# Two graph layers on one core: the check of group sizes moves to GpSimd between the passes, row numbers move to the drain, first-pass gathers wait only for their buffer

## The chip, the cores and the metric

One core of a Trainium2 chip runs the program. Its engines are TensorE (PE, with weight loads shown apart as PEld), VectorE (DVE), ScalarE (ACT), GpSimd (POOL) and SyncE (SP); each runs its own list of instructions and waits for the others on semaphores. ACT and SP also issue DMAs (ACTq, SPq), and GpSimd issues the gathers, which are DMAs that take their row numbers from a tile. The metric is the device time of one execution in microseconds, as the median of several.

## What is computed

100,000 nodes with 64 features, 50,000 edges with 32 attributes, edges given as `src` and `dst`, `dst` ascending.

```python
h = relu(layernorm(x))                                   # only x's shape matters to layer 0 here
# layer 0: over the edges of each src node
seg_sum, seg_max = segment_sum(edge_attr, src), segment_max(edge_attr, src)
seg_mean = seg_sum / max(cnt, 1);  seg_max = where(cnt > 0, seg_max, 0)
x = x + relu(concat[seg_sum, seg_max, seg_mean, u[0]] @ W1 + b1) @ W2 + b2
# layer 1
h = relu(layernorm(x))
x = x + relu(segment_sum(h[src], dst) @ W.T + b)
```

## The kernel before

**Before the passes** (0 to 186 us of the trace) the edges' `src` numbers are sorted on VectorE, the sorted positions are turned into row numbers for the gathers (`gi[0]`), and rows of flags for the scans are stored.

**The first pass** (layer 0) goes over 98 blocks (`BLOCKS`) of 512 sorted edges. For block n: GpSimd gathers the edges' attributes into a ring of eight buffers `xa` (`gather_attr`, four gathers of 128 rows, L540). VectorE multiplies them by a share (`scale_attr`, L1060), TensorE turns them (`turn_attr`, L1355), VectorE runs two scans over them (`scans`, L1072 and L1074), TensorE multiplies by W1 (L1360), ScalarE applies relu (`hidden`, L677), TensorE multiplies by W2 (L1367), VectorE writes the record (`less_constant`, L1122), ScalarE stores it in DRAM. Two blocks later SP and ACT load windows of 112 records for groups of 128 nodes (`windows` on SP, `upper_windows` on ACT, L667); VectorE copies their keys into PSUM (`keys_to_psum`, L1085) and makes 0/1 matrices (`onehots`, L1095), TensorE adds records up by node with them (`expand`, L1379, after one or two matmuls of ones that only fill time, L1384), and VectorE adds the node's own row (`add_dense`, L1114). SP stores the result as the table T.

These steps are software-pipelined by hand. VectorE's loop runs n from 0 to 104; its body at n is: scans(n), add_dense(n-7), keys_to_psum(n-5), scale_attr(n+2), onehots(n-5), less_constant(n-1). So from n = 98 on there is nothing left to scan, and the last seven bodies are the **drain**. When every row of T is stored, SP raises `table_ok`.

**The second pass** (layer 1) gathers rows of T by `gi[1]` (`gather_x`, L559), in the same manner, and ends the program. It is one arm of a choice: `fast` is 1 where no group has more than 112 edges and the row bounds hold; the other arm is a slow way for other inputs, not taken here. All five engines read `fast` before the second pass.

**What the choice needs.** `start_f` and `near_f` are rows of 800 group starts on one partition, for `src` and `dst`. From them `group_starts` (L839) makes the first pass's window addresses, `dst_group_starts` (L829 to L834) the second pass's, `start_row[1]`, and its share of the checks; `group_checks` (L844 to L848) is the rest of the checks. They stand in VectorE's loop at n = 3, 10 and 13. `permute(gi[1], 3, 7)` at n = 9 (L877 to L880) turns `src` numbers into T's row numbers. At n = 15 VectorE sums the counts of wrong items, TensorE adds them over the partitions (L1398), and VectorE writes `fast` (L1157).

**What paces the gathers.** `gather_attr(n)` waits at its first gather until buffer n-8 has been turned. Its second gather also waits for the scans of block n-4 (`feats_ok`), its third and fourth for `added` and `hot_ok` of earlier blocks.

## Time and profile before

| what | us |
|---|---|
| median of 3 runs (lowest, highest) | 1256.63 (1252.74, 1262.65) |
| the profiled execution | 1261.67 |
| its span in the trace | 1259.8 |
| VectorE busy in the span | 1030.1 (82%) |
| TensorE busy | 960.6 (76%) |
| GpSimd busy | 758.0 (60%) |
| ScalarE busy | 280.1 (22%) |
| TensorE's granted clock, mean (share of full) | 0.888 |

The span is the time from the first to the last event that the trace shows; the execution's own time is 1.9 us longer. A share over the whole span mixes four stages: sorting (0 to 186 us), the first pass (186 to 699), its drain (699 to 731) and the second pass (731 to 1260). Each must be read by itself. In rows of the timeline, a bracket gives the idle time of the engine ahead of the instruction and what ended it; "issue" means that nothing the profile shows was waited for.

### The profile page before, as it was taken

How to read it: one execution, taken by the hardware profiler on the slowest of the kernel's cores; microseconds unless marked ns; L12 is line 12 of the kernel's file. 1: busy time of each engine (PE TensorE's matmuls, PEld its weight loads, DVE VectorE, ACT ScalarE, POOL GpSimd, SP SyncE). 2: the span in 40 equal slices, each digit the busy share in tenths (PEclk: the TensorE clock that was granted, in tenths of full speed). 3: DMA queues.
4: the chain of work that ended last, by engine and by line, in shares of the span. 5: the costliest groups of instructions: out<-in, count | busy, mean ns of one | idle time of the engine just before them, and what ended most of it. 6: DMA issues, size and time to landing. Idle time of an engine off the chain costs nothing.

```text
span 1259.8 us, 20767 instructions
## 1 busy us (share of the span) xinstructions
PE 960.6 (76%) x5818; PEld 758.0 (60%) x5818; DVE 1030.1 (82%) x2727; ACT 280.1 (22%) x681; POOL 758.0 (60%) x821
## 2 busy tenths in 40 slices
PE   0131027979999999999999823879889788888888
PEld 0010014757777777777777613767767677677777
DVE  8888887899999999999999624777777777777774
ACT  1441042212222222222222101112112112111110
POOL 3000046667777777777776067777777777777750
PEclk9995556889999999999999955898999989988899
DMA  2000012767899888888888654777788778777775
GB/s 65 0 0 0 0 53 68 175 161 206 236 232 240 234 226 219 241 220 236 230 222 240 164 173 98 180 201 203 210 222 207 202 198 210 210 208 201 203 186 156
DMA packets 317563, 218.51 MB, mean 173 GB/s; under 512 B 223428, under 2 KB 255140, under 8 KB 317444
## 3 DMA queue, kind: packets, MB, share of 16 engines
q1 hardware_dynamic: 182100, 135.41, 38.7%
q10 hardware_dynamic: 110256, 62.42, 18.8%
q0 software_dynamic: 25088, 19.32, 8.6%
q8 instruction: 47, 0.77, 0.3%
q14 instruction: 72, 0.59, 0.1%
HBM read 137.51 MB, written 79.45 MB: 172 GB/s over the span
## 4 chain that ended last, share of the span: by engine, by line
DVE 36%; POOL 20%; DMA 13%; PE 11%; issue 10%; ACTq 5%; ACT 2%; SPq 0%; POOLq 0%; DVEq 0%
POOL xa L559 11%; POOL xa L540 9%; DMA xa<-node_table,gi 8%; DMA win<-records 5%; DVE feats L1074 4%; DVE feats L1072 4%; ACTq L667 3%; DVE oneh L1095 3%; DVE dout L1114 2%; PE p_m L1367 2%; DVE kb L920 2%; DVE ka L920 2%; DVE shared L1095 2%; DVE ka L921 2%; DVE kb L921 2%
## 5 line engine op out<-in xcount | busy, mean ns | idle before, releaser
L540 POOL DMA_INDIRECT xa<-in_edge_attr_dram,gi x392 | 375.2, 957 | 252.3 <-issue 115.4
L559 POOL DMA_INDIRECT xa<-node_table,gi x392 | 369.9, 944 | 158.7 <-issue 105.8
L677 ACT ACTIVATE hid<-p_z,bias_z 128x512 f32<-128x512 f32 x98 | 113.4, 1157 | 249.2 <-issue 230.0
L1408 PE MATMUL p_g<-ident,hn 128*128 128x128 f32 x196 | 46.6, 325 | 106.9 <-DVE hn L1182 106.5
L1074 DVE TENSOR_TENSOR_SCAN feats<-c_rows,feats,p_g 32x512 f32<-32x512 f32 x97 | 123.3, 1271 | 1.4
L1095 DVE SCALAR_TENSOR_TENSOR shared<-p_m,node_of 112x1024 f32<-112x1024 f32 x98 | 117.1, 1195 | 6.8 <-PE p_z L1379 3.4
L1072 DVE TENSOR_TENSOR_SCAN feats<-c_rows,feats,p_g 64x512 f32<-64x512 f32 x97 | 122.5, 1263 | 0.1
L1367 PE MATMUL p_m<-w_s,hid 128*128 128x64 f32 x784 | 109.3, 284 | 15.8 <-ACT hid L677 15.4
L730 ACT ACTIVATE sd<-mv,eps_t 128x4 f32<-128x4 f32 x98 | 29.1, 297 | 413.2 <-DVE mv L1173 350.4
L1095 DVE SCALAR_TENSOR_TENSOR oneh<-p_m,node_of 112x1024 f32<-112x1024 f32 x98 | 119.3, 1217 | 0.2
L1360 PE MATMUL p_z<-feats,w_s 96*128 96x512 f32 x196 | 112.4, 657 | 6.2 <-DVE feats L1074 6.2
L1168 DVE BATCH_NORM_STATS2 stat<-xa 128x6 f32<-128x64 f32 x392 | 58.7, 212 | 67.6 <-DMA xa<-node_table,gi 63.9
L1379 PEld LDWEIGHTS p_u<-win,oneh 128*128 128x128 f32 x784 | 97.1, 195 | 26.9 <-issue 22.5
L1384 PE MATMUL p_t<-one 128*128 128x256 f32 (+1 forms) x228 | 112.5, 578 | 0.0
L1379 PEld LDWEIGHTS p_t<-win,oneh 128*128 128x128 f32 x784 | 96.4, 194 | 25.5 <-issue 24.1
L1384 PE MATMUL p_u<-one 128*128 128x512 f32 x230 | 110.7, 566 | 0.0
L1367 PEld LDWEIGHTS p_m<-w_s,hid 128*128 128x128 f32 x784 | 97.6, 196 | 21.5 <-ACT hid L677 19.9
L1379 PE MATMUL p_u<-win,oneh 128*128 128x64 f32 x784 | 94.9, 275 | 2.2 <-DVE oneh L1095 2.2
L1408 PEld LDWEIGHTS p_g<-ident,hn 128*128 128x128 f32 x196 | 25.0, 159 | 117.8 <-DVE hn L1182 116.9
L1085 DVE COPY p_m<-win 112x8 f32<-112x8 f32 x196 | 32.8, 167 | 75.9 <-DMA win<-records 75.7
L1379 PE MATMUL p_t<-win,oneh 128*128 128x64 f32 x784 | 93.9, 273 | 0.5 <-DVE oneh L1095 0.5
L1182 DVE SCALAR_TENSOR_TENSOR hn<-xa,mv,p_m 128x64 f32<-128x64 f32 x392 | 83.9, 276 | 3.5
(253 smaller groups left out, 1539.3 us busy)
## 6 DMA issues: line engine op xcount, KB each, us to landing
win<-records SPq DMA_DIRECT2D x980, 28.9 KB
records<-rec ACTq DMA_DIRECT2D x196, 132.0 KB
din<-in_x_dram SPq DMA_DIRECT2D x49, 512.0 KB
node_table<-dout SPq DMA_DIRECT2D x49, 512.0 KB, 3.6
din<-node_table SPq DMA_DIRECT2D x43, 512.0 KB
out_dram<-dout SPq DMA_DIRECT2D x43, 512.0 KB
c_rows<-rows_src ACTq DMA_DIRECT2D x141, 128.0 KB
win<-records ACTq DMA_DIRECT2D x588, 28.9 KB
```

The source lines that it names most:

```text
L540: g.indirect_dma_start(out=xa[n % XRING][:, t, 0:FE], out_offset=None, in_=edge_attr, in_offset=bass.IndirectOffsetOnAxis(ap=gi[0][:, BT * ...
L559: g.indirect_dma_start(out=xa[k % XRING][:, t, :], out_offset=None, in_=T, in_offset=bass.IndirectOffsetOnAxis(ap=gi[1][:, BT * n + t:BT * ...
L677: s.activation(hid[n % 2][:, :].rearrange("p (t n) -> p n t", n=P), p_z[n % 2][:, :].rearrange("p (n t) -> p n t", t=BT), ACT.Relu, bias=b ...
L1072: v.tensor_tensor_scan(f[0:64, :], c[0:64, at:at + BLK], p_g[n % 2][0:64, :], first[0:64], ALU.mult, ALU.add)
L1074: v.tensor_tensor_scan(f[64:96, :], c[64:96, at:at + BLK], p_g[n % 2][0:32, :], first[64:96], ALU.min, ALU.max).then_inc(feats_ok, 1)
L1095: v.scalar_tensor_tensor(hots[side][m % HRING][0:WP, :, :], key_at(k).unsqueeze(2).to_broadcast([WP, PER, UNIT]), -float(STEP * m), node_o ...
L1182: last = v.scalar_tensor_tensor(hn[n % 2][:, t, :], xa[(BLOCKS + n) % XRING][:, t, :], mv[n % 2][:, t, 0:1], up[:, t:t + 1].to_broadcast([ ...
L1360: mm(p_z[n % 2][:, :], w1_s[:, :], feats[n % 2][:, :], start=True, stop=True).then_inc(z_ok, 1)
L1367: last = mm(p_m[0][:, D * t:D * (t + 1)], hid[n % 2][:, P * t:P * (t + 1)], w2_s[:, :], start=True, stop=True)
L1379: last = mm(to[:, D * s:D * (s + 1)], hots[side][m % HRING][:, s, :], win[k % WRING][:, s, 0:D], start=True, stop=True)
L1384: mm(bank[:, 0:width], one[:, :], one[:, :].unsqueeze(1).to_broadcast([P, width // P, P]), start=True, stop=True)
L1408: last = tr(p_g[n % 2][:, P * h:P * (h + 1)], hn[n % 2][:, 2 * h:2 * h + 2, :].rearrange("p t d -> p (t d)"), ident[:, :])
```

## The change

- The waits of `gather_attr` for `feats_ok`, `added` and `hot_ok` go. The wait for the buffer stays.
- `dst_group_starts` and `group_checks` go from VectorE. After its last first-pass gather has landed and after the preset of `hot1`, GpSimd now makes `over`, `over2` and `start_row[1]` from `start_f`, `near_f` and `limit` in 15 instructions of one partition by 800 or 784, each waiting for the one before, and raises `s_over`.
- `permute(gi[1], 3, 7)` moves on VectorE from n = 9 to n = 99.
- The choice moves from n = 15 to n = 101 (`CHOICE`), on VectorE and on TensorE. On VectorE it now begins with a wait for `s_over` and two sums over 784 numbers.

```diff
+CHOICE = BLOCKS + 3
             def gather_attr(n):
-                behind = n - LEAD
                 for t in range(BT):
                     if t == 0 and n >= XRING:
                         pool.wait_ge(turned, n - XRING + 1)
-                    if t == 1 and valid(behind):
-                        pool.wait_ge(feats_ok, behind + 1)
-                    elif t == 2 and valid(behind - SRC_ADD):
-                        pool.wait_ge(added, behind - SRC_ADD + 1)
-                    elif t == 3 and valid(behind - SRC_HOT):
-                        pool.wait_ge(hot_ok, behind - SRC_HOT + 1)
...
+            pool.wait_ge(s_near, 2)
+            pool.wait_ge(s_cast, 2)
+            for side, (row, more) in enumerate(((start_f, over), (near_f, over2))):
+                link(g.tensor_scalar(room[:, :], row[:, :], float(-ROW), None, ALU.mult))
+                link(g.tensor_tensor(room[:, :], room[:, :], limit[:, :], ALU.add))
+                link(g.tensor_scalar(more[:, :], room[:, :], 0.0, None, ALU.is_lt))
+                if side == 1:
+                    link(g.tensor_scalar(room[:, :], room[:, :], 0.0, None, ALU.max))
+                    link(g.tensor_tensor(room[:, :], limit[:, :], room[:, :], ALU.subtract))
+                    link(g.tensor_copy(start_row[1][:, :], room[:, :]))
+                link(g.tensor_tensor(room[:, 0:LAST], row[:, 1:LAST + 1], row[:, 0:LAST], ALU.subtract))
+                link(g.tensor_scalar(room[:, 0:LAST], room[:, 0:LAST], float(WP), None, ALU.is_gt))
+                last = g.tensor_tensor(more[:, 0:LAST], more[:, 0:LAST], room[:, 0:LAST], ALU.add)
+                if side == 0:
+                    link(last)
+            last.then_inc(s_over, 1)
             pool.wait_ge(s_fast, 1)
...
+            def choice():
+                dve.wait_ge(s_over, 1)
+                v.reduce_sum(wrong[0:1, 0:1], over[:, 0:LAST], AX.X)
+                v.reduce_sum(wrong[0:1, 1:2], over2[:, 0:LAST], AX.X)
+                v.tensor_scalar(wrong[0:1, 4:5], start_f[:, LAST:LAST + 1], float(E), None, ALU.not_equal)
+                link(v.tensor_scalar(wrong[0:1, 5:6], near_f[:, LAST:LAST + 1], float(E), None, ALU.not_equal))
+                v.reduce_sum(wrong1[:, :], wrong[:, :], AX.X).then_inc(s_wrong, 1)
+                dve.wait_ge(s_wsum, 1)
+                v.tensor_scalar(fast[:, :], p_m[1][0:1, 0:1], 0.0, None, ALU.is_equal).then_inc(s_fast, 1)
...
-                if n == 9:
+                if n == 3:
+                    group_starts()
+                if n == BLOCKS + 1:
                     dve.wait_ge(s_dcols, 16)
                     permute(gi[1], 3, 7)
                     v.tensor_copy(rowmax[:, :], eps_t[:, :]).then_inc(s_drows, 1)
-                if n == 3:
-                    group_starts()
-                if n == 10:
-                    dst_group_starts()
-                if n == 13:
-                    group_checks()
-                if n == 15:
-                    v.reduce_sum(wrong1[:, :], wrong[:, :], AX.X).then_inc(s_wrong, 1)
-                    dve.wait_ge(s_wsum, 1)
-                    v.tensor_scalar(fast[:, :], p_m[1][0:1, 0:1], 0.0, None, ALU.is_equal).then_inc(s_fast, 1)
+                if n == CHOICE:
+                    choice()
...
-                if n == 15:
+                if n == CHOICE:
                     pe.wait_ge(s_wrong, 1)
```

The order of GpSimd's instructions in the middle of the first pass, before the change; `xa3` to `xa4` are buffers of the ring, and the bracket names the semaphore waited for:

```order
L540 DMA xa3<-in_edge_attr_32_dram,gi0 128x32 [waits turned]
L540 DMA xa3<-in_edge_attr_32_dram,gi0 128x32 [waits feats_ok]
L540 DMA xa3<-in_edge_attr_32_dram,gi0 128x32 [waits added]
L540 DMA xa3<-in_edge_attr_32_dram,gi0 128x32 [waits hot_ok]
L540 DMA xa4<-in_edge_attr_32_dram,gi0 128x32 [waits turned]
L540 DMA xa4<-in_edge_attr_32_dram,gi0 128x32 [waits feats_ok]
L540 DMA xa4<-in_edge_attr_32_dram,gi0 128x32 [waits added]
L540 DMA xa4<-in_edge_attr_32_dram,gi0 128x32 [waits hot_ok]
```

The same place with the change:

```order
L536 DMA xa3<-in_edge_attr_32_dram,gi0 128x32 [waits turned]
L536 DMA xa3<-in_edge_attr_32_dram,gi0 128x32 x3
L536 DMA xa4<-in_edge_attr_32_dram,gi0 128x32 [waits turned]
L536 DMA xa4<-in_edge_attr_32_dram,gi0 128x32 x3
L536 DMA xa5<-in_edge_attr_32_dram,gi0 128x32 [waits turned]
L536 DMA xa5<-in_edge_attr_32_dram,gi0 128x32 x3
```

Three of four waits are gone; the one for the buffer stands.

VectorE's instructions from body 99 to body 102 of its loop, with the change (L1117 is the adding of the node's row, L1088 the copy of keys, L1098 the 0/1 matrix, L1125 the record):

```order
L1117 TENSOR_TENSOR dout<-p_t,din 128x512 [waits dense_out0_1,dense_in0_0,expanded]
L1088 COPY p_m<-win 112x8 [waits win_in_2]
L1098 SCALAR_TENSOR_TENSOR oneh<-p_m,node_of 112x1024 [waits window_keys_in_psum]
L880 TENSOR_SCALAR tm<-gi 128x512 [waits dst_columns]
L881 TENSOR_SCALAR td<-gi 128x512
L882 SCALAR_TENSOR_TENSOR gi<-gi,tm 128x512 [waits vector_step]
L883 TENSOR_TENSOR gi<-gi,td 128x512 [waits vector_step]
L1152 COPY rowmax<-eps_t 128x1 [waits vector_step]
L1117 TENSOR_TENSOR dout<-p_u,din 128x512 [waits expanded]
```

```order
L1098 SCALAR_TENSOR_TENSOR oneh<-p_m,node_of 112x1024 [waits window_keys_in_psum]
L845 TENSOR_REDUCE wrong<-over 1x1 [waits groups_checked]
L846 TENSOR_REDUCE wrong<-over 1x1
L847 TENSOR_SCALAR wrong<-start_f 1x1
L848 TENSOR_SCALAR wrong<-near_f 1x1
L849 TENSOR_REDUCE wrong<-wrong 128x1 [waits vector_step]
L851 TENSOR_SCALAR fast<-p_m 1x1 [waits wrong_summed]
L1117 TENSOR_TENSOR dout<-p_u,din 128x512 [waits expanded]
L1088 COPY p_m<-win 112x8 [waits win_in_1]
```

The first piece is the permutation behind the 0/1 matrix of block 94, the second the choice behind that of block 96. Before the change these places held only L1114, L1085 and L1095.

TensorE's last instructions of the first pass with the change (L1381 fills time, L1376 is the adding up by node, of blocks 95, 96 and 97):

```order
L1381 MATMUL p_u<-one 128x512
L1376 MATMUL p_u<-win,oneh 128x64 x8
L1395 MATMUL p_m<-one,wrong 1x1
L1381 MATMUL p_t<-one 128x512
L1376 MATMUL p_t<-win,oneh 128x64 x8
L1381 MATMUL p_u<-one 128x512
L1376 MATMUL p_u<-win,oneh 128x64 x8
```

The sum over the partitions (L1395) now stands between the adding up of blocks 95 and 96, and nothing behind it on TensorE can begin until VectorE has counted.

## Rows read from the trace of the kernel before

**Rows 1.** Stages: busy us (instructions) of PE, PEld, DVE, ACT, POOL, PEclk, DMA share, GB/s

```profile
295.00:456.00 161.00, 160.54 (x1045) 125.55 (x1043) 159.42 (x228) 44.33 (x65) 121.08 (x128) 1.00 0.90 233
699.00:731.00 32.00, 24.01 (x146) 18.41 (x144) 16.71 (x25) 3.97 (x5) 0.21 (x1) 0.89 0.66 181
```

**Rows 2.** Timeline of VectorE, first scan of blocks 8, 9, 17, 97: start us, us

```profile
236.62 1.26 DVE L1072 TENSOR_TENSOR_SCAN feats<-c_rows,feats,p_g 64x512 f32<-64x512 f32 x1
241.55 1.26 DVE L1072 TENSOR_TENSOR_SCAN feats<-c_rows,feats,p_g 64x512 f32<-64x512 f32 x1
...
295.14 1.26 DVE L1072 TENSOR_TENSOR_SCAN feats<-c_rows,feats,p_g 64x512 f32<-64x512 f32 x1
...
699.07 1.26 DVE L1072 TENSOR_TENSOR_SCAN feats<-c_rows,feats,p_g 64x512 f32<-64x512 f32 x1
```

**Rows 3.** Timeline of VectorE, what stands in bodies 9 to 15 besides the loop

```profile
246.47 0.47 DVE L877 TENSOR_SCALAR tm<-gi 128x512 int32<-128x512 int32 x1
...
248.75 0.15 DVE L1147 COPY rowmax<-eps_t 128x1 f32<-128x1 f32 x1
...
253.80 0.97 DVE L829 SCALAR_TENSOR_TENSOR start_row<-near_f,limit 1x800 int32<-1x800 f32 x1
...
257.59 0.96 DVE L833 TENSOR_REDUCE wrong<-over 1x1 f32<-1x784 f32 x1
...
289.82 0.15 DVE L1157 TENSOR_SCALAR fast<-p_m 1x1 int32<-1x1 f32 x1 [0.28 <-PE p_m L1398]
```

**Rows 4.** A stage of 4 us, columns as in rows 1

```profile
280.00:284.00 4.00, 3.04 (x7) 1.74 (x8) 3.97 (x7) 0.00 (x0) 2.22 (x3) 0.54 0.66 164
```

**Rows 5.** Timeline of TensorE and of VectorE, after the checks

```profile
280.96 2.07 PE L1360 MATMUL p_z<-feats,w_s 96*128 96x512 f32 x2 [2.29 <-DVE feats L1074]
```

```profile
269.03 0.42 DVE L1122 TENSOR_TENSOR rec<-p_m,c_neg 128x256 f32<-128x256 f32 x1 [0.67 <-PE p_m L1367]
...
289.05 0.42 DVE L1122 TENSOR_TENSOR rec<-p_m,c_neg 128x256 f32<-128x256 f32 x1 [1.09 <-PE p_m L1367]
```

**Rows 6.** Waits of GpSimd, 165 to 700 us: total, times, longest

```profile
POOL xa L540 <- DVE feats L1074: 24.0, 21, 4.2
```

**Rows 7.** Timeline of GpSimd: first and last first-pass gather, preset, first second-pass gathers

```profile
170.87 1.16 POOL L540 DMA_INDIRECT xa<-in_edge_attr_dram,gi  x1 [112.92 <-ACT gi L697]
...
684.47 0.95 POOL L540 DMA_INDIRECT xa<-in_edge_attr_dram,gi  x1 [0.30 <-issue]
689.21 2.13 POOL L570 COPY shared<-ident 32x1024 f32<-32x1024 f32 x2 [3.79 <-issue]
730.79 0.97 POOL L559 DMA_INDIRECT xa<-node_table,gi  x1 [39.46 <-SPq L416]
```

**Rows 8.** Timeline of VectorE: the multiplication by the share

```profile
477.12 0.29 DVE L1060 TENSOR_TENSOR xa<-xa,share 128x128 f32<-128x128 f32 x1 [0.47 <-DMA xa<-in_edge_attr_dram,gi]
...
690.88 0.60 DVE L1060 TENSOR_TENSOR xa<-xa,share 128x128 f32<-128x128 f32 x1
```

**Rows 9.** Timeline of GpSimd at the start

```profile
4.38 1.41 POOL L496 IOTA limit_i<- 1x800 int32 x1
...
15.90 0.35 POOL L517 TENSOR_SCALAR_AFFINE_SELECT shifted<-shifted 128x130 f32<-128x130 f32 x1
```

**Rows 10.** Timeline of the drain, VectorE and then TensorE

```profile
717.09 1.22 DVE L1095 SCALAR_TENSOR_TENSOR oneh<-p_m,node_of 112x1024 f32<-112x1024 f32 x1
...
721.86 0.17 DVE L1085 COPY p_m<-win 112x8 f32<-112x8 f32 x1 [2.95 <-DMA win<-records]
```

```profile
718.37 2.00 PE L1379 MATMUL p_t<-win,oneh 128*128 128x64 f32 x16 [0.51 <-DVE oneh L1095]
720.20 1.08 PE L1384 MATMUL p_u<-one 128*128 128x512 f32 x2
723.35 3.08 PE L1379 MATMUL p_u<-win,oneh 128*128 128x64 f32 x16 [2.07 <-DVE oneh L1095]
```

**Rows 11.** The page's costliest groups: second-pass gathers

```profile
L559 POOL DMA_INDIRECT xa<-node_table,gi x392 | 369.9, 944 | 158.7 <-issue 105.8
```

More of the change, by code:

```diff
@@ L178, in build @@
         near_f = sb("near_f", [1, GROUPS])
+        room = sb("room", [1, GROUPS])
         wrong = sb("wrong", [P, 6])
@@ L238, in build @@
         s_wrong = sem("wrong_counted")
+        s_over = sem("groups_checked")
         s_wsum = sem("wrong_summed")
@@ L823, in rows_above @@
                 v.tensor_tensor(in_group[:, :], less[:, 1:SPAN + 1], less[:, 0:SPAN], ALU.subtract).then_inc(s_above, 1)
-            def dst_group_starts():
-                dve.wait_ge(s_near, 1)
-                dve.wait_ge(s_cast, 2)
-                v.scalar_tensor_tensor(start_row[1][:, :], near_f[:, :], float(ROW), limit[:, :], ALU.mult, ALU.min)
-                v.scalar_tensor_tensor(over2[:, :], near_f[:, :], float(ROW), limit[:, :], ALU.mult, ALU.is_gt)
-                link(v.tensor_tensor(over[:, 0:LAST], near_f[:, 1:LAST + 1], near_f[:, 0:LAST], ALU.subtract))
-                link(v.scalar_tensor_tensor(over[:, 0:LAST], over[:, 0:LAST], float(WP), over2[:, 0:LAST], ALU.is_gt, ALU.add))
-                link(v.reduce_sum(wrong[0:1, 1:2], over[:, 0:LAST], AX.X))
-                link(v.tensor_scalar(wrong[0:1, 5:6], near_f[:, LAST:LAST + 1], float(E), None, ALU.not_equal))
             def group_starts():
@@ L839, in group_starts @@
                 v.scalar_tensor_tensor(start_row[0][:, :], start_f[:, :], float(ROW), limit[:, :], ALU.mult, ALU.min).then_inc(s_start, 1)
-            def group_checks():
-                last = LAST
-                link(v.scalar_tensor_tensor(over2[:, :], start_f[:, :], float(ROW), limit[:, :], ALU.mult, ALU.is_gt))
-                link(v.tensor_tensor(over[:, 0:last], start_f[:, 1:last + 1], start_f[:, 0:last], ALU.subtract))
-                link(v.scalar_tensor_tensor(over[:, 0:last], over[:, 0:last], float(WP), over2[:, 0:last], ALU.is_gt, ALU.add))
-                v.reduce_sum(wrong[0:1, 0:1], over[:, 0:last], AX.X)
-                link(v.tensor_scalar(wrong[0:1, 4:5], start_f[:, last:last + 1], float(E), None, ALU.not_equal))
+            def choice():
[7 more added lines that the diff above has]
+                v.tensor_scalar(fast[:, :], p_m[1][0:1, 0:1], 0.0, None, ALU.is_equal).then_inc(s_fast, 1)
             def beside_turn(t):
```

## The prediction

> **What bounds the kernel now.** I read the busy time by stages first. In the clean part of the first pass (295 to 456 us) VectorE is busy 159.4 of 161 us, at full TensorE clock, while TensorE shows 160.5 and GpSimd 121.1 [rows 1]. TensorE's figure counts overlapping ends and matmuls that only fill time, so it does not decide; the timeline does: VectorE begins block 9's scan 4.93 us after block 8's [rows 2], back to back, and that is the loop's period. From block 17 to block 97 it takes 403.9 us, 5.05 us a block [rows 2]: 80 x 4.93 = 394.4, so 9.5 us are stalls spread over that stretch. From block 9 to block 17, eight blocks, it takes 53.6 us where 39.4 would do [rows 2]: 14.2 us too much. The code that the change moves stands in this stretch. Of GpSimd, 392 gathers at 0.94 us and a gap of 0.30 (the bracket of its rows) are about 1.25 us each, 5.0 us a block, a little slower than VectorE's 4.93. It took from 170.87 to 685.4 [rows 7], 514.5 us, of which 24.0 in 21 waits for VectorE's scans [rows 6]; each of those would have had the ordinary gap of 0.3 anyway, so 17.7 us are real waiting.
>
> The second pass begins at `table_ok`: the first gather stands at 730.79 [rows 7]. There GpSimd is idle 158.7 us in all for 392 gathers, 39.5 of it ahead of the first [rows 7, 11]; the other 119.2 us are 0.30 us a gather, the plain gap. So it issues without ever truly waiting, and the second pass starts and ends later or earlier as a whole with `table_ok`.
>
> **The work that leaves the loop.** The permutation runs from 246.47 to the end of its small copy at 248.9: 2.4 us. The six instructions for `near_f` run from 253.80 to 258.55 and one small one of 0.15: 4.9 us. The five for `start_f` are four of 0.96 us and a small one: 4.0 us. The choice is two of 0.15 and a wait of 0.28, 0.6 us [rows 3]. Together 11.9 us. VectorE also lost 0.67 us at 269.03 and 1.09 us at 289.05 waiting for TensorE [rows 5]. These I count as consequences: while VectorE checks, TensorE has no scan to multiply, stands idle 2.29 us, and then runs at a mean granted clock of 0.54 (nearly all at the 1.2 GHz level), the pair of L1360 taking 2.07 us [rows 4, 5]. Without the checks it has no such gap. 11.9 + 1.8 is 13.7 of the 14.2; the remaining 0.5 has the same neighbourhood. I take **-14.2 us**; if the slow-clock waits stayed, -11.9.
>
> **The gathers.** They now wait for nothing but a buffer turned eight blocks ago. At 5.0 us a block from 170.87 GpSimd would be done at 661 to 668, instead of 685.4, and its rows landed some 3.8 us later (685.4 to the preset at 689.2, which waits for them) [rows 7]: by 672 at the latest. VectorE needs block 97's rows at 690.88 [rows 8], 15 us sooner with the savings, at about 676. So GpSimd stays ahead to the end, by 4 us or more, and no buffer wait arises, since it is never eight blocks ahead. What this removes on VectorE's side is waits like the 0.47 us at 477.12 [rows 8] and what follows from them; I count **-1.0**, between 0 and -1.5. Most of the 9.5 us of stalls are not waits for gathers and I leave them where they are. The loop's saving would be lost in part without this edit: gathers at 5.0 us a block that also wait for scans have only the slack of rows 8.
>
> **The check on GpSimd.** 15 instructions on one partition, none of which the trace shows. Bounds for one: the preset's copy, 1,024 elements in half of 2.13 us [rows 7], is 0.83 us for 800; the slowest per element is L517, 130 elements in 0.35 us, which is 2.15 us for 800 [rows 9]. The one row of this very shape, one partition by 800, is L496's 1.41 us [rows 9]; I take it, 15 x 1.41 = 21 us (12 to 32). They start when the last gather has landed (667 to 672) and the preset's 2.1 us are over, so `s_over` comes at about 690 to 695. VectorE asks for it after block 96's 0/1 matrix, which ended at 718.3 [rows 10] and now ends at 703. It is hidden, by 8 us or more; it begins to cost where one instruction takes over about 2.2 us, so the cover holds on the whole range but barely at its end.
>
> While these run, VectorE still multiplies by the share for the last two blocks. In rows 8 this instruction took 0.60 us instead of 0.29, at 690.88, beside the second of the two copies of rows 7, and ended about when the copy did; the scans beside them kept their 1.26 to 1.27. Two such instructions, each held for about half of a 1.0 to 1.4 us instruction, less the 0.31 paid now: **+0.7** (0 to +2). The Trainium skill states this, in "SBUF — State Buffer", section "Who interferes with whom": a VectorE instruction with both inputs in SBUF contends with a GpSimd instruction that reads SBUF, and one with at most one input there does not. By that rule, the trace agrees: 0.60 against 0.29 for the one, no change for the scans, which read PSUM.
>
> **The drain.** The permutation comes in after block 94's matrix, in a place where VectorE waits for windows anyway: at most 0.6 us late for the next, made good by the wait for the window of block 96; **+0.1**. The choice comes at 718.3 (old clock): two sums of 0.96, three small ones, a matmul and its wait: about 3.0 us until `fast`. On VectorE that fills the 2.95 us of waiting for block 97's window [rows 10] and costs 0.1. TensorE pays more. It ran block 96's adding up at 718.37, in 2.00 us, and filled time at 720.20, so that block 97's could begin at 723.35 [rows 10]. Now block 96 must wait for the count, until about 720.9, with an idle gap of 3.4 us ahead. Then come fill (0.9), 16 matmuls (1.8), fill (0.9), 16 matmuls (1.9), ending at 726.4: at full clock nothing is lost against 723.35 + 3.08 = 726.43. If TensorE is at half clock throughout, it is 1.7 + 3.1 + 1.7 + 3.1 = 9.6 us, ending at 730.5, +4.1. A shorter gap, 2.29 us, was followed by the low clock [rows 4, 5], so I put it nearer that end: **+2.7** (0.1 to 4.1). Reading `fast` is late too, but `table_ok` is another 7 us behind.
>
> **Sum.** -14.2 - 1.0 + 0.7 + 0.1 + 2.7 = **-11.7 us**. The profiled execution had 1261.67 us, so 1250.0 for it; it stood 5.0 us above the median of the runs, 1256.63, and against that the time is **1245 us**, 0.9% faster. The ends of the terms (-11.9 or -14.2; 0 or -1.5; 0 or 2; 0.2 or 4.2) make -15.5 to -5.7, that is 1241 to 1251.
>
> **Rivals.**
> (a) *The spread stalls go too.* The 9.5 us of stalls after block 17 may come from gathers that arrive just in time: in rows 8 a wait for a gather stands among them, and the stretch 295 to 456, with the gathers ahead, has almost none (159.4 of 161 us busy). With GpSimd ahead throughout, 8 us more would go: 1237. Against it: I see most of them as late records, behind ScalarE's issue of window loads.
> (b) *The earlier gathers bring stalls to where there were none.* They come at other moments, and the DMA share is already 0.90 [rows 1]. Stalls at the rate of the second half (some 7 us in 43 blocks) over the 32 clean ones would cost 5 us: 1250.
> (c) *Slower.* The count comes late and holds the drain. The time is lost one for one from 2.2 us an instruction on; the gain is used up at 2.2 + 11.7/15 = 3.0 us, and at 3.85 us, 58 us for the 15, the time is over 1% longer, 1269. For it: nothing like these instructions is in the trace. Against it: it would have to be nearly twice the dearest row.
> The Trainium skill, "GPSIMD Engine Reference", section "Performance versus the Vector engine", speaks against putting elementwise work there, about twice VectorE's time; its 4497 ns for 2,048 elements of two inputs would be 1.76 us for 800, an estimate of 26 us if all 15 cost that. By it the count is ready at about 700, still ahead of 703, and the sum stays; that rule makes (c) thin cover but no loss. No run here shows it yet.
> (d) *Nothing comes of it*: the stretch from block 9 to 17 is held by something else once the checks are gone, GpSimd or ScalarE's issue. Then some 3 us remain: 1253. Rows 2's 4.93 us a block right before it speak against.
>
> **How the numbers follow.** Forecast 0.52, (a) 0.17, (b) 0.18, (c) 0.04, (d) 0.09. About 1% (12.6 us, below 1244.1) is what a measurement can tell from no change. The forecast's 1241 to 1251 lies a third below it; (a) wholly: faster 0.4. Slower than 1269 only in (c)'s far end: 0.03. Same: 0.57. The range reaches from (a) to beyond (b): **1237 to 1254**.
>
> **What would show it.** Right: first scans of blocks 9 to 17 take about 39.5 us; no TensorE clock below 1.0 there; GpSimd's last first-pass gather ends by 668; its checks are over before VectorE's 0/1 matrix of block 96; no wait of L845 for them; a gap of about 3.4 us and slow matmuls on TensorE in the drain; `table_ok` about 12 us sooner, the second pass as long as before (529 us). Wrong: VectorE waiting at L845; L1060's successor waiting for gathers; stalls before block 60.

## The result and the profile after

The changed kernel takes 1248.95 us (median of 15 runs, 1243.64 to 1255.75) against 1257.42 for the kernel before (15 runs, 1252.74 to 1262.89): a ratio of 0.9924, with a 95% interval of 0.9907 to 0.9942. It is 0.8% faster, 9.6 us by the ratio (7.3 to 11.7 by the interval) and 8.5 between the medians. That is less than the 1% which the prediction had taken as its bound, but the interval does not reach 1. Two further timings of the changed kernel, below, gave 0.9931 and 0.9918. Differences in us between timed kernels are worked out from the ratios here.

The profiled execution took 1251.71 us with a span of 1249.8; of before it was 1261.67 and 1259.8. Stages are cut at first scans and at the first second-pass gather. The third column of the table is another execution of the changed kernel, profiled later; its span is nearer to the usual one.

| us | before | changed | changed, third timing |
|---|---|---|---|
| start to block 9's scan | 241.6 | 241.4 | 240.4 |
| block 9 to 17 | 53.6 | 42.3 | 40.2 |
| block 17 to 97 | 403.9 | 401.7 | 401.0 |
| block 97 to the first second-pass gather (drain) | 31.7 | 36.2 | 35.7 |
| from there to the end | 529.0 | 528.2 | 528.2 |
| span | 1259.8 | 1249.8 | 1245.5 |

The timeline of VectorE of the changed kernel (start us, us), first scans of blocks 9, 17 and 97, answers [rows 2]:

```profile
241.39 1.26 DVE L1075 TENSOR_TENSOR_SCAN feats<-c_rows,feats,p_g 64x512 f32<-64x512 f32 x1
...
283.68 1.26 DVE L1075 TENSOR_TENSOR_SCAN feats<-c_rows,feats,p_g 64x512 f32<-64x512 f32 x1
...
685.43 1.26 DVE L1075 TENSOR_TENSOR_SCAN feats<-c_rows,feats,p_g 64x512 f32<-64x512 f32 x1
```

GpSimd's timeline of the same execution, last first-pass gather to first second-pass gather, answers [rows 7] and shows some of the new instructions:

```profile
662.16 1.09 POOL L536 DMA_INDIRECT xa<-in_edge_attr_dram,gi  x1 [0.30 <-issue]
666.75 2.13 POOL L566 COPY shared<-ident 32x1024 f32<-32x1024 f32 x2 [3.50 <-issue]
668.97 2.23 POOL L571 TENSOR_SCALAR room<-start_f 1x800 f32<-1x800 f32 x1
671.28 1.87 POOL L572 TENSOR_TENSOR room<-room,limit 1x800 f32<-1x800 f32 x1
...
675.53 1.48 POOL L578 TENSOR_TENSOR room<-start_f 1x784 f32<-1x784 f32 x1
677.09 2.17 POOL L579 TENSOR_SCALAR room<-room 1x784 f32<-1x784 f32 x1
...
692.01 0.84 POOL L577 CAST start_row<-room 1x800 int32<-1x800 f32 x1
...
696.75 1.84 POOL L580 TENSOR_TENSOR over<-over,room 1x784 f32<-1x784 f32 x1
721.62 1.06 POOL L555 DMA_INDIRECT xa<-node_table,gi  x1 [23.03 <-SPq L419]
```

Gathers end 22 us earlier than in [rows 7] and wait for no scan any more. The chain of 15 runs from 668.97 to 698.59, 29.6 us. The choice, on VectorE, and then TensorE around it, same execution, answer [rows 10]:

```profile
705.71 0.95 DVE L845 TENSOR_REDUCE wrong<-over 1x1 f32<-1x784 f32 x1
...
713.44 0.69 DVE L1117 TENSOR_TENSOR dout<-p_t,din 128x512 f32<-128x512 f32 x1 [3.22 <-PE p_t L1376]
```

```profile
703.91 2.27 PE L1376 MATMUL p_u<-win,oneh 128*128 128x64 f32 x16 [1.25 <-DVE oneh L1098]
707.91 0.19 PE L1395 MATMUL p_m<-one,wrong 128*1 128x1 f32 x2 [1.73 <-DVE wrong L849]
708.02 2.07 PE L1381 MATMUL p_t<-one 128*128 128x512 f32 x2
709.89 3.51 PE L1376 MATMUL p_t<-win,oneh 128*128 128x64 f32 x16
```

TensorE stands idle for the count (1.73 us), then takes 3.51 us for 16 matmuls that took 2.00 in [rows 10], and VectorE waits 3.22 us for them. The windows of these stages (from:to, us, busy us of PE, PEld, DVE, ACT, POOL, granted clock, DMA share, GB/s) say why, and answer [rows 1, 4]:

```profile
272.00:276.00 4.00, 4.00 (x14) 2.15 (x12) 3.95 (x7) 1.15 (x1) 3.09 (x4) 0.57 0.90 200
706.00:714.00 8.00, 6.27 (x22) 4.67 (x22) 4.42 (x10) 1.28 (x1) 0.00 (x0) 0.50 0.60 206
```

A granted clock of 0.50 is the 1.2 GHz level for the whole of 706 to 714.

The 2.9 us that block 9 to 17 takes over 39.4 in this execution come from ScalarE's queue (start us, us):

```profile
267.35 2.01 ACTq L679 DMA_DIRECT2D win<-records  x2
269.41 1.15 ACT L689 ACTIVATE hid<-p_z,bias_z 128x512 f32<-128x512 f32 x1 [3.57 <-issue]
```

```profile
271.75 0.42 DVE L1125 TENSOR_TENSOR rec<-p_m,c_neg 128x256 f32<-128x256 f32 x1 [0.92 <-PE p_m L1364]
...
278.27 0.42 DVE L1125 TENSOR_TENSOR rec<-p_m,c_neg 128x256 f32<-128x256 f32 x1 [1.50 <-PE p_m L1364]
```

The two window issues took 2.01 us where they take 0.82 to 0.86 a block before and after, relu started late behind them, TensorE had a gap of 1.06 and ran 272 to 276 at a mean clock of 0.57, and VectorE waited 0.92 and 1.50 us. Eight other executions below, of kernels with the checks and the permutation out of this stretch and nothing else changed in it, took 39.5 to 40.2; so this was chance. The sign of being right that asked for no lowered clock there holds in the second and third profile of the changed kernel (1.00 in every window of 4 us) and not in this one.

### The profile page after: what moved, and what is told of

Read it like the earlier page. It is cut to its first block, busy times and chain, and to the rows that moved or that the text cites. A ratio compares the mean times of both kernels' runs of the same rounds, so it can differ in the third digit from the quotient of the medians.

```text
span 1249.8 us, 20773 instructions
## 1 busy us (share of the span) xinstructions
PE 968.8 (78%) x5818; PEld 765.5 (61%) x5818; DVE 1024.1 (82%) x2720; ACT 280.4 (22%) x681; POOL 784.5 (63%) x836
## 4 chain that ended last, share of the span: by engine, by line
DVE 47%; PE 16%; DMA 12%; POOL 9%; issue 7%; ACTq 6%; ACT 3%; DVEq 0%; POOLq 0%; SPq 0%
POOL xa L555 9%; DMA xa<-node_table,gi 7%; DVE feats L1077 7%; DVE feats L1075 7%; DVE oneh L1098 5%; DMA win<-records 4%; DVE dout L1117 4%; ACTq L679 4%; PE p_m L1364 3%; DVE kb L923 2%; DVE rec L1125 2%; DVE ka L923 2%; DVE shared L1098 2%; PE p_u L1376 2%; PE p_t L1376 2%
## 5 line engine op out<-in xcount | busy, mean ns | idle before, releaser
L1075 DVE TENSOR_TENSOR_SCAN feats<-c_rows,feats,p_g 64x512 f32<-64x512 f32 x97 | 122.5, 1263 | 0.0
L1098 DVE SCALAR_TENSOR_TENSOR shared<-p_m,node_of 112x1024 f32<-112x1024 f32 x98 | 117.2, 1196 | 3.8 <-PE p_u L1376 1.4
L1098 DVE SCALAR_TENSOR_TENSOR oneh<-p_m,node_of 112x1024 f32<-112x1024 f32 x98 | 119.3, 1217 | 0.2
L1381 PE MATMUL p_u<-one 128*128 128x512 f32 x230 | 115.9, 590 | 0.1
L1376 PEld LDWEIGHTS p_u<-win,oneh 128*128 128x128 f32 x784 | 96.2, 193 | 26.7 <-issue 24.6
L1381 PE MATMUL p_t<-one 128*128 128x256 f32 (+1 forms) x228 | 112.4, 578 | 0.0
L1376 PEld LDWEIGHTS p_t<-win,oneh 128*128 128x128 f32 x784 | 96.9, 195 | 24.0 <-issue 24.0
L1376 PE MATMUL p_u<-win,oneh 128*128 128x64 f32 x784 | 93.6, 273 | 1.3 <-DVE oneh L1098 1.3
L1376 PE MATMUL p_t<-win,oneh 128*128 128x64 f32 x784 | 94.4, 274 | 0.0
L1088 DVE COPY p_m<-win 112x8 f32<-112x8 f32 x196 | 32.8, 168 | 70.8 <-DMA win<-records 70.6
```

The costliest lines, as they stand in the source:

```text
L1075: v.tensor_tensor_scan(f[0:64, :], c[0:64, at:at + BLK], p_g[n % 2][0:64, :], first[0:64], ALU.mult, ALU.add)
L1098: v.scalar_tensor_tensor(hots[side][m % HRING][0:WP, :, :], key_at(k).unsqueeze(2).to_broadcast([WP, PER, UNIT]), -float(STEP * m), node_o ...
L1376: last = mm(to[:, D * s:D * (s + 1)], hots[side][m % HRING][:, s, :], win[k % WRING][:, s, 0:D], start=True, stop=True)
L1381: mm(bank[:, 0:width], one[:, :], one[:, :].unsqueeze(1).to_broadcast([P, width // P, P]), start=True, stop=True)
```

## The experiments

Ratios are against the kernel before, timed beside it on the same chip. There were three such sets of timings; the kernel before had 1259.23, 1262.37 and 1260.53 us. Each kernel is the changed one with one edit, unless said.

**Are the gathers' waits worth anything, and by what?** First the waits put back:

```diff
+                    if t == 1 and valid(n - LEAD):
+                        pool.wait_ge(feats_ok, n - LEAD + 1)
+                    elif t == 2 and valid(n - LEAD - SRC_ADD):
+                        pool.wait_ge(added, n - LEAD - SRC_ADD + 1)
+                    elif t == 3 and valid(n - LEAD - SRC_HOT):
+                        pool.wait_ge(hot_ok, n - LEAD - SRC_HOT + 1)
```

> The changed kernel with the gathers' waits for scans, adding and 0/1 matrices put back; all else as changed. My theory: the removal of these waits is worth little by itself once VectorE's checks are gone, because VectorE's 4.93 us a block is the bound and what stalls remain are late records behind ScalarE's slow issue of window loads. But GpSimd then ends its gathers some 20 us later, at about 682 instead of 663, and its 29.6 us chain of checks (measured in the changed kernel, 668.97 to 698.59) would end near 718, when VectorE asks for it at 706: a wait of about 12 us at L845 in the drain. So: loop as in the changed kernel within 3 us, drain 10 to 13 us longer, 1258 to 1263 in all, about the time of the kernel before or slower. Rival, that the waits cost nothing and their removal only tidies: 1249, no wait at L845. Rival, that unpaced gathers cause the stalls: the loop gets shorter by 3 us or more with the waits back.

Then the kernel before without them (no other edit):

> The kernel before with nothing changed but the gathers' waits for scans, adding and 0/1 matrices removed. My theory: removes only VectorE's waits for gathers and what follows (0.4 + 0.47 us and the stalls behind them); -1 to -3 us, 1254 to 1256.5, with GpSimd's last gather ending near 665 instead of 685, and blocks 9 to 17 still 53 us. Rival, that late gathers are behind most of the 9.5 us of stalls after block 17: -6 to -9 us, 1249 to 1251. Rival, that gathers running ahead cause stalls: slower by 3 us or more.

Measured: waits back 1253.63 us, 0.9948 (0.9924 to 0.9972); only the waits off 1258.55, 0.9998 (0.9968 to 1.0028). By itself this edit is worth nothing that the timing shows (it would show 3.8 us), though the last gather starts at 665.14 in place of 684.47. With the waits back it starts at 671.62, the chain is over at 708.38, and VectorE's timeline (matrix of block 96, then the count) has what rival (c) described:

```profile
702.86 1.22 DVE L1104 SCALAR_TENSOR_TENSOR oneh<-p_m,node_of 112x1024 f32<-112x1024 f32 x1
708.42 0.96 DVE L851 TENSOR_REDUCE wrong<-over 1x1 f32<-1x784 f32 x1 [4.33 <-POOL over L586]
```

The drain then takes 40.6 us in place of 35.0 to 36.2. So the edit's use is that the chain of checks starts 9 us sooner. The profiles show this; the timing does not by itself, since 0.9948 and the changed kernel's 0.9924, 0.9931 and 0.9918 lie within each other's intervals or next to them. The wait at the count is 4.3 us where I had expected about 12, and the time lies below the expected 1258 to 1263: I had put the last gather later, at 682; but VectorE's scans, for which they waited, come 14 us sooner too.

**How much cover has the chain?** Nine more instructions of one partition by 800 ahead of `s_over`, which nobody reads:

```diff
-            last.then_inc(s_over, 1)
+            link(last)
+            for _ in range(8):
+                link(g.tensor_scalar(room[:, :], near_f[:, :], float(-ROW), None, ALU.mult))
+            g.tensor_scalar(room[:, :], near_f[:, :], float(-ROW), None, ALU.mult).then_inc(s_over, 1)
```

> The changed kernel with nine more GpSimd instructions of the kind of L571 (2.2 us each in the changed kernel) ahead of the signal that the groups are checked; they write a tile nobody reads any more. The chain took 29.6 us and ended 7.1 us before VectorE asked. Nine more make it about 50 us. Theory, that the cover is these 7 us and not more: VectorE waits 13 to 14 us at L845, TensorE with it, total +13 to +15 us, 1262 to 1264. Rival, that table_ok hides it (13 us lie between the choice and the first gather): +4 or less.

Measured: 1268.57 us, 1.0054 (1.0031 to 1.0077), 1.2% or 15.5 us more than the changed kernel in the same set (0.9931). VectorE's timeline:

```profile
700.88 1.22 DVE L1101 SCALAR_TENSOR_TENSOR oneh<-p_m,node_of 112x1024 f32<-112x1024 f32 x1
721.33 0.96 DVE L848 TENSOR_REDUCE wrong<-over 1x1 f32<-1x784 f32 x1 [19.23 <-POOL room L586]
```

Some 20 us of chain gave 19.2 us of waiting and a drain of 54.5: in this profile time is lost one for one, and the cover is under 1 us, not the 7 us that the changed kernel's first profile shows (chain over at 698.59, asked for at 705.71). The timing alone does not decide it: 15.5 us, give or take 4.7, is also what I had expected from a cover of 7 us. The changed kernel, profiled again, does:

> The changed kernel as it is, beside the others of this call, as their base. By the first three profiles of its relatives, its own 42.3 us from block 9 to 17 was chance (39.5 to 39.7 in the three others that have the checks out of the loop), so here that stretch should be 39.4 to 40 us, and the drain 36 us again. Rival: the stretch is 42 us again, which would make it a property of this kernel.

> The changed kernel as it is, beside the three others of this call, as their base: 9 to 17 in 39.5 to 42.3 us, 17 to 97 in 400 to 402, drain 35 to 36, second pass 528 to 529; ratio to the kernel before 0.991 to 0.994.

Measured: 1251.57 us, 0.9931 (0.9902 to 0.9960), and 1247.85, 0.9918 (0.9887 to 0.9948). GpSimd's timeline of the last, its end, and VectorE's at the same place:

```profile
693.02 1.94 POOL L577 CAST start_row<-room 1x800 int32<-1x800 f32 x1
695.05 1.81 POOL L578 TENSOR_TENSOR room<-near_f 1x784 f32<-1x784 f32 x1
696.94 2.49 POOL L579 TENSOR_SCALAR room<-room 1x784 f32<-1x784 f32 x1
699.52 1.84 POOL L580 TENSOR_TENSOR over<-over,room 1x784 f32<-1x784 f32 x1
```

```profile
694.30 1.22 DVE L882 SCALAR_TENSOR_TENSOR gi<-gi,tm 128x512 int32<-128x512 int32 x1
695.55 1.86 DVE L883 TENSOR_TENSOR gi<-gi,td 128x512 int32<-128x512 int32 x1
...
701.39 0.96 DVE L845 TENSOR_REDUCE wrong<-over 1x1 f32<-1x784 f32 x1
```

The chain ends at 701.36 and the sum begins at 701.39. Here the moved permutation meets the chain: its two last instructions take 1.22 and 1.86 us instead of 0.69 each, and GpSimd's beside them 1.94, 1.81 and 2.49 instead of 0.84, 1.48 and 2.17. In the first profile VectorE was later (the stalls at 271 and 278), the permutation began as the chain ended (698.49), and nothing was lengthened. Four kernels with the same chain and another edit in the drain, where VectorE asks between 700.6 and 702.1, had 1.3 to 3.0 us of cover. So it is between 0 and 3 us wherever VectorE is not late.

**Is the permutation well placed?** Put back into body 9:

```diff
-                if n == BLOCKS + 1:
+                if n == 9:
                     dve.wait_ge(s_dcols, 16)
                     permute(gi[1], 3, 7)
```

> The changed kernel with the permutation of gi[1] back in body 9 of VectorE's loop (bodies 10, 13 and 15 stay empty). Theory: its 2.4 us stand on VectorE's path in the loop and on nobody's in the drain, so the stretch from block 9 to 17 goes from 39.5 to 41.9 us, the drain loses 0 to 0.6, total +1.8 to +2.4 us against the changed kernel (0.15 to 0.2% of it). Rival, that an insertion in the loop costs more than its own time because TensorE idles and falls to the low clock, as I took for the two checks: +4 us or more. Rival, that it costs nothing in either place: 0.

Measured: 1250.22 us, 0.9910 (0.9877 to 0.9943), not told apart from the changed kernel beside it (0.9931). Blocks 9 to 17 took 42.1 us instead of 39.5, as costed; the drain took 36.8. 2.6 us are 0.2% and too little for these intervals, and the drain was not shorter without it; so whether its place matters is not shown.

In the drain the permutation is not free for TensorE, though. In the changed kernel's third profile, TensorE waits 1.76 us for VectorE's adding of the node's row, which stands behind the permutation, and its clock is low from there on:

```profile
698.25 2.08 PE L1381 MATMUL p_u<-one 128*128 128x512 f32 x2 [1.76 <-DVE dout L1117]
700.12 3.51 PE L1376 MATMUL p_u<-win,oneh 128*128 128x64 f32 x16
703.60 0.19 PE L1395 MATMUL p_m<-one,wrong 128*1 128x1 f32 x2
```

So there the 16 matmuls of block 95 already ran at the 1.2 GHz level (granted clock 0.50 from 699 to 711), the count was ready before they ended, and TensorE did not stand idle for it at all; the drain was 35.7 us all the same. The kernel with the permutation in body 9 has no such wait; TensorE stands idle 3.96 us for the count instead.

**Was it the checks on VectorE that cost, and are they worth the move to GpSimd?** `dst_group_starts` and `group_checks` back on VectorE at n = 10 and 13, the 15 instructions gone, permutation and choice in the drain:

> The changed kernel with the group checks and start_row[1] made by VectorE in bodies 10 and 13 again, as before the change; choice (without its two sums) and permutation stay in the drain, the gathers unpaced. Theory: the stretch from block 9 to 17 takes 39.5 + 8.9 us of checks + about 2 us for the idle gaps and low clock of TensorE that two inserts of 4 and 5 us bring (before: 53.6 with the permutation's 2.4 and the choice's 0.6 in it), 50 to 51; the choice in the drain is shorter by the two sums (1.9 us), so TensorE's gap and with it the drain shrink, 33 to 35 us. Total +7.5 to +10 us against the changed kernel. Rival, that the inserts cost only their own time, 48.4 us. Rival, that the move to GpSimd brings nothing since something else binds the stretch: under +3.

Measured: 1254.74 us, 0.9949 (0.9927 to 0.9970), beside 0.9918 for the changed kernel: 4 us more, give or take 4.7 (the two half widths, 0.0022 and 0.0030, added in squares). Expected were 7.5 to 10 us more and 50 to 51 us for blocks 9 to 17. These took 53.0: 39.5, 8.9 of checks, and 4.6 more, of which 4.4 are waits for TensorE, in two rows of VectorE:

```profile
268.46 0.42 DVE L1124 TENSOR_TENSOR rec<-p_m,c_neg 128x256 f32<-128x256 f32 x1 [2.69 <-PE p_m L1367]
...
275.19 0.42 DVE L1124 TENSOR_TENSOR rec<-p_m,c_neg 128x256 f32<-128x256 f32 x1 [1.71 <-PE p_m L1367]
```

So the knock-on belongs to the checks: with the permutation alone there was none. TensorE's granted clock fell to 0.50 in this stretch with the checks in it, to 0.73 in one window of 4 us with the permutation alone, and with neither it stayed at 1.00, the chance stall aside. The drain was 33.9 us against 35.7. The two spans differ by 13.2 us. The 8.9 of checks less the 1.8 that the drain is shorter would be 7.1, which the timing allows; the full 13.2 it does not, and this kernel's profiled execution, 1260.65 us, lay 5.9 above its median. So an ordinary execution probably has less of the knock-on than this one. The kernel with only the waits off bears this out: profiled at 1258.75, beside its median of 1258.55, it took 53.6 us for blocks 9 to 17, the same as the kernel before, and waited 2.1 us for records there.

**Can the choice be made cheaper in the drain?** First the sum over partitions one block later on TensorE, into a bank that is free there, and `fast` written two bodies after the count:

```diff
                 v.reduce_sum(wrong1[:, :], wrong[:, :], AX.X).then_inc(s_wrong, 1)
+            def write_fast():
                 dve.wait_ge(s_wsum, 1)
-                v.tensor_scalar(fast[:, :], p_m[1][0:1, 0:1], 0.0, None, ALU.is_equal).then_inc(s_fast, 1)
+                v.tensor_scalar(fast[:, :], p_g[0][0:1, 0:1], 0.0, None, ALU.is_equal).then_inc(s_fast, 1)
...
                 if n == CHOICE:
                     choice()
+                if n == CHOICE + 2:
+                    write_fast()
...
-                if n == CHOICE:
+                if n == CHOICE + 1:
                     pe.wait_ge(s_wrong, 1)
```

> The changed kernel, with TensorE's sum over the partitions one place later, behind the adding up of block 96, and fast written by VectorE two bodies later (into and from another PSUM bank). VectorE's count stays in body 101. Theory, that the drain's loss (36.2 us from block 97's scan to the first gather against 31.7 before) comes from TensorE standing idle ahead of the sum and then running both last blocks at a low granted clock: TensorE works on block 96 at once, the drain falls back to 32 to 33 us, total -3 to -4.5 against the changed kernel, 1244.5 to 1246. Rival, that the loss is VectorE's count itself or the permutation (2 to 3 us of work in the drain): no change, 1249, within 1 us.

> The same kernel as in the run with the sum behind block 96, again, beside the changed kernel itself. Its drain was 32.5 us against 35.0 and 36.2, so it should be 2.5 to 3.7 us faster than the changed kernel (0.2 to 0.3%), at a ratio of 0.988 to 0.991 to the kernel before. Rival, that the drain's gain is given back in the second pass: the same ratio as the changed kernel's, and a second pass longer than 528 to 529 us.

Measured: 1247.44 us, 0.9899 (0.9862 to 0.9936), and in the third set 1246.24, 0.9894 (0.9862 to 0.9926), beside 0.9918 for the changed kernel. TensorE's timeline of the first:

```profile
702.15 1.08 PE L1386 MATMUL p_t<-one 128*128 128x512 f32 x2
703.07 1.89 PE L1381 MATMUL p_t<-win,oneh 128*128 128x64 f32 x16
704.89 0.19 PE L1400 MATMUL p_g<-one,wrong 128*1 128x1 f32 x2
705.01 1.12 PE L1386 MATMUL p_u<-one 128*128 128x512 f32 x2
707.16 2.00 PE L1381 MATMUL p_u<-win,oneh 128*128 128x64 f32 x16 [1.03 <-DVE oneh L1101]
```

Block 96 is added up while VectorE counts, in 1.89 us, and the sum comes right behind it without a wait. The drain takes 32.5 and 33.8 us instead of 35.0 to 36.2. This is the fastest kernel of the study, 1.0% below the kernel before; against the changed kernel its 0.2 to 0.3% is seen in both timings, but the intervals overlap.

Then three pairs of filling matmuls ahead of TensorE's wait, to keep its clock up:

```diff
                 if n == CHOICE:
+                    for _ in range(3):
+                        stream(p_g[0], BLK)
                     pe.wait_ge(s_wrong, 1)
```

> The changed kernel with three matmul pairs of ones (into the free bank p_g0) ahead of TensorE's wait for the count, so that TensorE is busy through the gap and the wait itself stays. If the loss in the drain is the low clock behind the gap (2.07 and 3.51 us for the fill and the 16 matmuls of block 96 against 1.02 and 1.89), most of it comes back: the wait ends at the same time, block 96 and 97 then take 0.9 + 1.8 + 0.9 + 1.9 = 5.5 us instead of 9.3, -3 to -3.8 us, 1245 to 1246. If it is the order alone (block 96 held behind the count), the gap's 1.7 us stay and nothing comes back: 1249 within 1 us.

> The kernel with three more matmul pairs ahead of TensorE's wait, again. Its drain was 33.3 us (changed: 35.0 and 36.2), but its second pass took 534.5 us where all others took 527.6 to 530.8, and its time was no better than the changed kernel's. If that was chance: second pass 528 to 530 us here and 1.7 to 2.9 us faster than the changed kernel. If a kernel whose TensorE is busier in the drain pays in the second pass: 532 us or more again.

Measured: 1251.08 us, 0.9918 (0.9884 to 0.9952), and 1248.92, 0.9913 (0.9880 to 0.9946): like the changed kernel. The two profiles show why it is not reliable. The first, then the second, on TensorE:

```profile
700.60 2.79 PE L1381 MATMUL p_g<-one 128*128 128x512 f32 x6
703.33 0.19 PE L1397 MATMUL p_m<-one,wrong 128*1 128x1 f32 x2
703.45 1.12 PE L1381 MATMUL p_t<-one 128*128 128x512 f32 x2
704.41 1.90 PE L1376 MATMUL p_t<-win,oneh 128*128 128x64 f32 x16
```

```profile
698.39 1.13 PE L1381 MATMUL p_u<-one 128*128 128x512 f32 x2 [1.75 <-DVE dout L1117]
699.73 2.92 PE L1376 MATMUL p_u<-win,oneh 128*128 128x64 f32 x16 [0.21 <-DVE oneh L1098]
702.44 5.27 PE L1381 MATMUL p_g<-one 128*128 128x512 f32 x6
707.64 0.19 PE L1397 MATMUL p_m<-one,wrong 128*1 128x1 f32 x2
```

In the first the clock was still full, the fill took 2.79 us, and blocks 96 and 97 ran at full speed (drain 33.3). In the second it had already fallen during block 95, the same six matmuls took 5.27 us, and the sum behind them came late: VectorE waited 4.20 us at `fast` (drain 36.7). In the first, the stretch from the first second-pass gather to the end took 534.5 us; in every other profile of the study it was 527.6 to 530.8, the second one with fills 528.1, so it was chance. The first profile says one thing more: the count still stood ahead of block 96, only the clock had stayed full, and the drain was 1.7 to 2.9 us shorter than the changed kernel's. So the low clock is a large part of what the order costs.

**What are the remaining stalls of the loop?** Many sit at the same blocks in most kernels (65, 69, 72, 73, 77, 81, 85, 95), nearly all as waits of VectorE for a record. In the first pass one window load of a block's eight moved from ScalarE's queue to SyncE's:

```diff
-SP_LOADS = (6, 4)
+SP_LOADS = (7, 4)
```

> The changed kernel with SP issuing seven of the first pass's eight windows a block and ScalarE one, instead of six and two. Theory on what is left of the stalls in the loop (some 7 to 9 us from block 17 to 97, all of them VectorE waiting 0.3 to 1.5 us for the record of L1125 in blocks where ScalarE's second window issue took 1 to 1.6 us instead of 0.4 ahead of its relu): they fall to a third, blocks 17 to 97 in 396 to 398 us instead of 400 to 402, total -3 to -5. Rival, that the issue on ScalarE is slow because the DMA queues are full: the wait moves to the one issue left or to SP, and nothing changes, or SP with 3.1 us of issues and 1.3 of loads a block becomes late and the loop gets slower.

Measured: 1283.11 us, 1.0178 (1.0141 to 1.0216), 2.5% above the changed kernel, where 3 to 5 us less were expected; blocks 17 to 97 took 430.6 us. Waits of VectorE between 295 and 700 us (engine line, waited for, us, times, longest), of the changed kernel's first profile and then of this one:

```profile
DVE rec L1125 <- PE p_m L1364: 8.6, 12, 2.7
```

```profile
DVE p_m L1088 <- DMA win<-records: 28.1, 26, 2.6
...
DVE rec L1125 <- PE p_m L1364: 0.8, 3, 0.4
```

The waits for records all but vanish, and 28.1 us of waits for windows come in: SyncE's queue now takes 3.2 us for seven issues in a row (median), where six took 2.75. So the spread stalls hang on ScalarE's issues, as far as this shows (a VectorE that waits elsewhere leaves TensorE time as well), and SyncE has no room to take one. Why now and then a single issue takes 1.0 to 1.6 us instead of 0.4 stays open.

## Why the prediction came out as it did

The forecast was 1245 us, 11.7 us less; measured were 9.6, 8.7 and 10.3 us less (0.9924, 0.9931 and 0.9918 of the kernel before). Range, sign and the most likely case (within 1%) held, and the forecast lies inside all three intervals, at the very edge of the first. Step by step:

- **The loop, -14.2.** Right. 39.5 to 40.2 us in eight of nine profiles of kernels with the checks and the permutation out of the stretch (the moved window load aside), where 39.4 was forecast; the ninth is the first profile's chance stall. Rival (d) is out. (Its price was summed wrongly too: without the -14.2 the other terms make +2.5, 1259 and not 1253.) That the waits for TensorE were a consequence of the checks, the weakest inference, the two rows of the kernel with the checks back bear out; the kernel with only the permutation back had none. The kernel with only the waits off had the same 53.6 us in an ordinary execution, so the -14.2 is no oddity of the one profile from which it was read.
- **The gathers, -1.0.** Too small to time (0.9998 alone, give or take 3.8 us). In the profiles, blocks 17 to 97 take 403.8 and 403.9 us in the two kernels with the waits and 399.1 to 402.4 in the eleven without (the one with the moved window load aside), so it is nearer -2.5. Its real role, starting the chain early, I had only touched in a half sentence; with the waits back the drain is 4.4 to 5.6 us longer.
- **The chain, 21 us, hidden by 8 us or more.** Wrong in size twice. It takes 29.6 to 31.4 us, so an instruction costs 2.0 us on average and not 1.41; the row of the same shape at the start (a sequence of numbers written, [rows 9]) was the wrong neighbour, and L517's rate, which gives 2.15 us, came close for the one-input form. The range 12 to 32 did hold it. And in the second and third profile VectorE asks at 701, where I had 703, because block 97's scan comes 17.5 us sooner there and not 15.2. The cover is 0 us in these two and up to 3 us in the relatives, so the limit of 2.2 us an instruction was too generous: at 2.0 to 2.1 there is nothing left, and a further microsecond of chain cost about one. The working had a slip as well: with its own latest start, 674, the limit is 29/15 = 1.9 us, and the upper end of 32 us is not covered. That the chain costs nothing all the same is partly luck.
- **Contention, +0.7.** Right in sum for the multiplication by the share in the first profile: 0.85 and 0.72 us in place of 0.28 (two instructions, beside GpSimd's copy and L572), 1.0 more, against 0.31 paid before. In the second they took 0.28 and 0.69, in the third 0.56 and 0.56, so it is 0.1 to 0.7 by the moment at which they meet. What I left out was that the permutation is of the same kind, and meets the chain too, and that GpSimd is lengthened in turn.
- **The permutation in the drain, +0.1.** On VectorE 1.7 us more where the chain runs beside it, and TensorE waits 1.75 to 1.77 us behind it in four profiles, which was not foreseen; whether that costs time is not shown.
- **The choice, +2.7.** Right in kind, too small in size, and not by the gap alone. The drain is 3.3 to 4.5 us longer in all, with 2.8 forecast for choice and permutation. The slow matmuls of block 96 are there in all three profiles of the changed kernel (3.51 us). But the idle gap for the count, forecast as 3.4 us, was 1.73, 2.02 and, in the third, none: there the clock had fallen before the count. Only the kernel with the permutation back in the loop has the gap that the rows gave, 3.96; these rows make it 3.9 and not 3.4, since block 95's adding up ended at 716.95. The sum one block later leaves a drain 1.2 to 3.7 us shorter, and a full clock with the old order 1.7 to 2.9; each takes most of the loss away in the profiles, so the order seems to cost mainly by way of the clock. In the timings neither is clear of noise.
- **The second pass moves as a whole.** Right: 527.6 to 530.8 in 13 of 14 profiles.
- **Rivals (a) and (b).** The spread stalls stayed (8.6 us of waits for records from 295 to 700 in the rows above, 7.1 before, where (a) wanted them gone). Between blocks 17 and 60 the changed kernel loses 1.0 to 1.7 us against 4.93 us a block, before it was 3.5; no new stalls came, so (b) is out too.

In the profiles the terms add up: -0.2 - 11.3 - 2.2 + 4.5 - 0.8 = -10.0, which is 1261.67 to 1251.71. Drain and gathers against their terms about cancel, or leave 1 us. The 1.4 to 3.0 us that are missing from the forecast are no more than the intervals allow for, so there may be nothing to explain; if there is, the drain is the one term that was clearly too small.

## What to carry

Work taken off a saturated engine pays in full there, with the waits that it caused for its partner; the same work on a slow engine is free only up to the moment at which the saved time itself brings the request forward, so the cover must be counted after the saving. Count a new dependency on TensorE by its place: one matmul that waits for a count belongs behind the work that could run meanwhile, which in the profiles here is worth 1.2 to 3.7 us of the drain without a single instruction less (the timings are too coarse for it). An idle TensorE may then cost more by its clock than by the gap, and what lowers the clock can be another wait than the one suspected. An edit that measures nothing alone (the gathers' waits) can be what another edit rests on, as the profiles show here.

## What the runs showed of the hardware

- **GpSimd's cost by form**, one partition by 800, f32: one-input multiply, compare or maximum 2.20 to 2.23 us, two-input 1.86 to 1.88, two shifted views of one row (784) 1.48, conversion to int32 0.84. The one-input form is the dearest. The Trainium skill, "GPSIMD Engine Reference", section "Performance versus the Vector engine", gives 4497 ns for 2,048 elements of two inputs, an estimate of 1.76 us for 800: the trace agrees, with 1.87. The table in section "Engine selection" of the same page of the Trainium skill has two-input operations about two times slower than on VectorE and one-input ones roughly at line-rate; the trace disagrees, with 2.20 us for one input, more than the 1.87 for two, and 0.96 for VectorE's operations on such rows [rows 3].
- **Who holds whom.** VectorE's L1063, both inputs in SBUF, takes 0.28 us alone; in the first profile it took 0.85 beside GpSimd's copy and 0.72 beside its two-input instruction, ending 0.1 to 0.2 us after them. Beside the one-input instruction it depended on the moment. Two pairs of rows, VectorE and GpSimd, of the changed kernel's first and third profile:

```profile
677.94 0.28 DVE L1063 TENSOR_TENSOR xa<-xa,share 128x128 f32<-128x128 f32 x1
```

```profile
674.22 2.21 POOL L573 TENSOR_SCALAR over<-room 1x800 f32<-1x800 f32 x1
```

```profile
674.65 0.56 DVE L1063 TENSOR_TENSOR xa<-xa,share 128x128 f32<-128x128 f32 x1
```

  At 677.94, 0.85 us into a one-input instruction (L579, 677.09), it was not held at all; at 674.65, 0.43 us into one, it was held until about 1.0 us after that one's start. Of nine such pairs, six that began 0.85 us in or later took 0.28 and three that began 0.43 to 0.53 in took 0.46 to 0.56. So GpSimd seems to hold back L1063 only in the first half of such an instruction, which is inferred, not tried, and need not hold for others: in the kernel with the waits back, the permutation's first instruction began 1.56 us into one and took 0.93 us instead of 0.42. The Trainium skill, "SBUF — State Buffer", section "Who interferes with whom", names the right instructions. It says of VectorE's two-port mode that whoever issues first has the ports for the whole instruction; if that went for L1063 too, it would wait to the end of GpSimd's, and the trace disagrees, with 0.28 us.
- **It works both ways.** GpSimd's conversion took 1.94 us instead of 0.84 beside the permutation, in the rows of the changed kernel's third profile above.
